# POOL's waits placed between shorter runs of the routing, and the second layer's bias products put into rounds of the expert loop

## The chip, the cores and the metric

The kernel runs on one core of one Trainium2 chip. The metric is the time of one execution in device microseconds; three runs are timed and the median counts. A profile is one execution recorded by the hardware profiler, with its own time. Engines are named as in the profile: PE (TensorE, matrix products), PEld (its weight loads), DVE (VectorE), ACT (ScalarE), POOL (GpSimd) and SP (SyncE, here only transfers and waits). All are programmed one by one and wait for each other through semaphores, counters that one engine raises and another waits on.

## What is computed

The input x is 128 x 125 x 64 (f32). Three stages follow one another; every number is f32 in the reference. Cut to what matters:

```python
h = tok(x)                        # depthwise conv, 5 taps, stride 2: 128 x 63 x 64; norm; leaky relu
h = h + attn(layernorm(h))        # selective scan, 16 states, along 63 positions
# third stage: 64 experts, 2 of them per token (8064 tokens)
xf = layernorm(h).reshape(-1, 64)
logits = xf @ Wr + br
topk_logits, topk_idx = top_k(logits, 2)
gates = softmax(topk_logits, axis=1)
combine = zeros(T, 64); combine[token, topk_idx] += gates
for e in range(64):
    y = relu(xf @ W1[e] + b1[e]) @ W2[e] + b2[e]
    out = out + combine[:, e:e + 1] * y
h = h + out
```

Since every y carries b2[e], the bias part of the output is `combine @ b2`, an 8064 x 64 by 64 x 64 product.

## The kernel before, in words

The first two stages take some 390 us and are not touched. The third one works on 63 tiles of 128 tokens, one tile per position. A tile has 128 rows of 64 numbers, one token in each partition.

**Routing.** The tiles are cut into groups of 8 (group 0 to 7) and into three shares: groups 0 and 1, groups 2 to 4, groups 5 to 7. For each group ACT normalises, PE transposes and multiplies by Wr (L762, L767), ACT copies the logits (L1117), DVE takes the two best experts (`choose`, L1504 to L1511, which raises s_hot). PE then counts tokens per expert (L807, L811; ACT copies the counts, L1123) and ranks each token within its expert (L823, L825, L833). At a share's end DVE works out where each expert's rows begin (`offsets_of`, s_off), PE adds these (L841, s_rank), and DVE turns ranks into row numbers, the slots (L1533 to L1547, s_slot). POOL then scatters the rows: for each tile and each of its two choices one indirect transfer (`send`, L630) writes 128 rows of the tile to `sorted_rows`, 126 transfers in all. They are numbered d = 0 to 125; share 0 has d = 0 to 31, share 1 d = 32 to 79, share 2 d = 80 to 125.

**The expert loop.** The sorted rows are padded to 40 units of 4 pairs of 128-row tiles. A step takes 2 pairs; there are 80 steps (24, 28 and 28 in the shares). In round k PE computes the output products of step k - 4 (L906), the hidden products of step k - 2 (L897) and the transposes of the rows of step k (L887), and then raises s_pstep. ACT and DVE wait for that round: ACT copies the transposed rows (L1162) and applies relu to half of the hidden part (L1167), DVE to the other half (L1595) and copies the outputs (L1604); they raise s_astep and s_dstep. PE's round k waits for their round k - 2. ACT stores the outputs of a step to `expert_out` (L1176); SP loads the weights of the pairs ahead into 23 places.

**The gathers.** For each tile and choice POOL fetches the 128 results by an indirect gather (L651), 126 in all, numbered d = 126 to 251; a share's gathers wait for all its stores. The last share's 46 gathers lie behind the loop. DVE then multiplies by the gates and adds (L1645, L1647), and SP writes the output.

**The bias part.** Beside the loop DVE builds the combine matrix (L1612, L1622). Behind the loop, for each of 8 groups q, PE transposes four 128 x 128 blocks of it (L940), ACT copies them (L1213), PE multiplies them by b2 (L931) and DVE adds the result to h (L1653, raising s_cbc).

**POOL's waits.** `keep_pace(d)` is called ahead of every indirect transfer. Three tables say where POOL waits: `GROUP_AT` (for s_hot, the choices of a group), `STEP_AT` (for a step of the loop, at every second transfer from d = 62 on, spread so that 153 transfers go with 80 steps) and `BIAS_AT` (for s_cbc, at every third transfer from d = 212 on). They set how POOL's transfers lie beside the other engines' work, and are not needed for the data.

Of the kernel before, what the change touches and what calls it, by code (L numbers as in the profile page):

```python
# [15 lines left out]
P = 128  # L16
T_IN = 125
C = 64
# [47 lines left out]
LAG_H, LATE = 2, 4  # L66
STEPS = [-(-n // 2) for n in PAIRS]
# [50 lines left out]
def groups_of(h):  # L118
    a, z = SHARES[h]
    return range(a // QG, -(-z // QG))  # L120

# [21 lines left out]
def build(nc, x, w, b, gamma, beta, alpha, A_log, D_param, scale, W_dt, b_dt, W_B, b_B, W_C, b_C,  # L143
# [5 lines left out]
    with ExitStack() as ctx:  # L149
# [88 lines left out]
        xT_e = x_w1[:, o:o + 4 * P].rearrange("p (k q n) -> p k q n", k=2, n=P)  # L238
        o += 4 * P
# [102 lines left out]
        s_comb = sem("s_comb")  # L342
        s_cT = sem("s_cT")
        s_cTc = sem("s_cTc")
        s_cb = sem("s_cb")
        s_cbc = sem("s_cbc")
# [112 lines left out]
        def _(pool):  # L459
# [197 lines left out]
        def _(pe):  # L657
# [223 lines left out]
            def rows_T(i):  # L881

                for j, n in enumerate(pairs_of(i)):
                    u = unit_of(n)
                    if in_share(n) % UNIT == 0:
                        pe.wait_ge(s_rows[u % RING], 16 * (u // RING + 1))
                    last = pe.transpose(ps[:, i % 2, j * P:(j + 1) * P], rows_in[:, u % RING, in_share(n) % UNIT, :],  # L887
                                        ident[:, :])
                return last

            def hidden(i):
# [3 lines left out]
                for j, n in enumerate(pairs_of(i)):  # L895
                    for t in range(2):
                        last = pe.matmul(ps[:, 2 + 2 * (i % 2) + t, j * P:(j + 1) * P],  # L897
                                         w_of(n)[t * C:(t + 1) * C, t, 0:HID],
                                         xT_e[t * C:(t + 1) * C, i % 2, j, :], start=True, stop=True)
# [10 lines left out]
            for k in range(STEP0[-1] + LATE):  # L910
                if k >= LAG_H:
                    pe.wait_ge(s_astep, k - LAG_H + 1)
# [3 lines left out]
                if LAG_H <= k < STEP0[-1] + LAG_H:  # L916
# [5 lines left out]
            pe.wait_ge(s_b2, 32)  # L922
            pe.wait_ge(s_dstep, dve_rounds(STEP0[-1]))

            def bias_of(q):

                pe.wait_ge(s_cTc, q + 1)
                if q >= 2:
                    pe.wait_ge(s_cbc, q - 1)
                for j in range(4):  # L930
                    last = pe.matmul(ps[:, 4 + q % 2, j * P:(j + 1) * P], cT[:, q % 2, j * P:(j + 1) * P], b2w[:, :],  # L931
                                     start=True, stop=True)
                last.then_inc(s_cb, 1)

            for q in range(CQ):
                pe.wait_ge(s_comb, q + 1)
                if q >= 2:
                    pe.wait_ge(s_cTc, q - 1)
                for j in range(4):
                    last = pe.transpose(ps[:, q % 2, j * P:(j + 1) * P],  # L940
                                        comb[0][:, 8 * q + 2 * j:8 * q + 2 * j + 2, :].rearrange("p l e -> p (l e)"), ident[:, :])
                last.then_inc(s_cT, 1)
                if q > 0:
                    bias_of(q - 1)
            bias_of(CQ - 1)

        @block.scalar
        def _(act):
# [210 lines left out]
            def xT_copy(i):  # L1159

                m = len(pairs_of(i))
                return act.activation(xT_e[:, i % 2, 0:m, :].rearrange("p q n -> p (q n)"), ps[:, i % 2, 0:m * P], ACT.Copy)  # L1162
# [23 lines left out]
            def next_rows(i):  # L1186

                d = i + 1
                u = d // (UNIT // 2) - 1 + RING
                if d % (UNIT // 2) == 0 and u < UNIT0[-1]:  # L1190
                    rows_of_unit(u)
# [3 lines left out]
            for k in range(STEP0[-1] + LAG_H):  # L1195
                act.wait_ge(s_pstep, k + 1)
                if k < STEP0[-1]:
                    last = xT_copy(k)
                if k >= LAG_H:
                    last = relu_A(k - LAG_H)  # L1200
                last.then_inc(s_astep, 1)
                if k < STEP0[-1]:
                    next_rows(k)
# [4 lines left out]

            for q in range(CQ):
                act.wait_ge(s_cT, q + 1)  # L1210
                if q >= 2:
                    act.wait_ge(s_cb, q - 1)
                act.activation(cT[:, q % 2, :], ps[:, q % 2, :], ACT.Copy).then_inc(s_cTc, 1)  # L1213

        @block.vector
        def _(dve):
# [401 lines left out]
            def both_gates(q):  # L1618
# [3 lines left out]
                dve.tensor_tensor(comb[0][:, span, :], comb[0][:, span, :], comb[1][:, span, :], ALU.add  # L1622
                                  ).then_inc(s_comb, 1)
# [59 lines left out]
```

## Time and profile before

| | us |
|---|---|
| median of 3 runs | 845.22 (843.47 to 846.76) |
| the profiled execution, its own time | 847.63 |
| its span | 845.7 |
| PE busy | 500.7 (59%) |
| DVE busy | 559.6 (66%) |
| ACT busy | 323.1 (38%) |
| POOL busy | 597.6 (71%) |

The mean granted TensorE clock was 0.778 of full speed. The span is the time from the first to the last instruction on the profiler's clock; the execution's own time is 1.9 us longer. In a row of the timeline the first number is the start in us from the span's start, the second how long it took; then come engine, line, operation, written tile, read tiles and shapes; x8 at the end means eight instructions in one row. In brackets stands how long the engine had been idle and what ended that. "remote" or "another core or an unknown queue" stands where no work was found that ended a wait; "issue" where no wait is seen. A PE product of f32 data shows as two passes, so 4 products show as x8; a transpose shows as one pass.

### The profile page before, as it was taken

How to read it: one execution, taken by the hardware profiler on the slowest of the kernel's cores; microseconds unless marked ns; L12 is line 12 of the kernel's file. 1: busy time of each engine (PE TensorE's matmuls, PEld its weight loads, DVE VectorE, ACT ScalarE, POOL GpSimd, SP SyncE). 2: the span in 40 equal slices, each digit the busy share in tenths (PEclk: the TensorE clock that was granted, in tenths of full speed). 3: DMA queues.
4: the chain of work that ended last, by engine and by line, in shares of the span. 5: the costliest groups of instructions: out<-in, count | busy, mean ns of one | idle time of the engine just before them, and what ended most of it. 6: DMA issues, size and time to landing. Idle time of an engine off the chain costs nothing.

```text
span 845.7 us, 8932 instructions
## 1 busy us (share of the span) xinstructions
PE 500.7 (59%) x2514; PEld 323.0 (38%) x2520; DVE 559.6 (66%) x1180; ACT 323.1 (38%) x622; POOL 597.6 (71%) x393
## 2 busy tenths in 40 slices
PE   4744245657558576556644675776886784777200
PEld 4733012222223122223423252665675673666100
DVE  1697899999999999997823564444544552333082
ACT  2159856555646655542310230222322331332000
POOL 5995779999999999992272357466666546654664
PEclk9968568798878879887756575799979895998555
DMA  7999970000000000000035102588888995852121
GB/s 251 382 183 121 77 3 0 1 0 0 0 0 0 0 0 0 0 0 0 8 91 141 30 19 89 148 230 248 234 254 234 250 289 133 232 148 58 23 84 51
DMA packets 106604, 84.95 MB, mean 100 GB/s; under 512 B 30464, under 2 KB 90240, under 8 KB 106560
## 3 DMA queue, kind: packets, MB, share of 16 engines
q1 hardware_dynamic: 79312, 54.76, 30.1%
q10 hardware_dynamic: 19184, 21.40, 8.6%
q0 software_dynamic: 8064, 8.27, 3.9%
q8 instruction: 19, 0.31, 0.2%
q14 instruction: 25, 0.20, 0.1%
HBM read 57.22 MB, written 33.49 MB: 107 GB/s over the span
## 4 chain that ended last, share of the span: by engine, by line
POOL 29%; PE 28%; issue 13%; DVE 11%; another core or an unknown queue 10%; ACT 6%; DMA 1%; ACTq 1%; POOLq 1%; DVEq 0%
POOL x_w L578 14%; POOL w_ring L571 10%; PE ps L906 10%; PE ps L897 6%; PE ps L887 5%; POOL xt L651 2%; PE ps L740 1%; PE ps L767 1%; PE ps L762 1%; DVE x_w L1595 1%; ACT xp L1102 1%; POOL hg L491 1%; POOL hh_ring L488 1%; DVE lstat L1290 1%
## 5 line engine op out<-in xcount | busy, mean ns | idle before, releaser
L740 PE MATMUL ps<-x_w,ident 128*128 128x512 f32 x252 | 154.9, 774 | 99.7 <-POOL x_w L578 99.7
L630 POOL DMA_INDIRECT sorted_rows<-xp,slot_i x126 | 122.4, 971 | 115.9 <-issue 34.7
L651 POOL DMA_INDIRECT xt<-expert_out,slot_i x126 | 121.9, 967 | 80.9 <-issue 31.7
L571 POOL TENSOR_TENSOR w_ring<-xt,bc 128x2016 f32<-128x2016 f32 x32 | 143.9, 4499 | 13.4 <-DVE hh_ring L1419 7.3
L1419 DVE TENSOR_TENSOR_SCAN hh_ring<-ps,w_ring 128x1024 f32<-128x1024 f32 x64 | 145.7, 2277 | 0.1
L578 POOL TENSOR_TENSOR x_w<-hh_ring,bc 128x2016 f32<-128x2016 f32 (+1 forms) x32 | 141.5, 4424 | 1.2 <-PE ps L740 1.2
L740 PEld LDWEIGHTS ps<-x_w,ident 128*128 128x128 f32 x252 | 60.5, 250 | 196.7 <-POOL x_w L578 122.6
L1162 ACT ACTIVATE x_w<-ps 128x256 f32<-128x256 f32 x80 | 30.8, 386 | 184.6 <-PE ps L887 129.1
L1072 ACT ACTIVATE ps<-dt_t,a_exp 128x1024 f32<-128x1024 f32 x64 | 71.5, 1117 | 64.3 <-DVE hh_ring L1419 64.3
L1066 ACT ACTIVATE ps<-dt_t,a_exp 128x1024 f32<-128x1024 f32 x64 | 71.5, 1118 | 51.2 <-DVE w_ring L1398 51.2
L1398 DVE TENSOR_TENSOR w_ring<-ps,w_ring 128x1008 f32<-128x1008 f32 x64 | 76.5, 1196 | 4.2 <-ACT ps L1066 4.2
L1413 DVE SCALAR_TENSOR_TENSOR w_ring<-ps,w_ring 128x1008 f32<-128x1008 f32 x64 | 75.5, 1179 | 0.0
L1595 DVE TENSOR_SCALAR x_w<-ps,x_w 128x128 f32<-128x128 f32 x56 | 17.3, 345 | 63.2 <-remote 31.6
L906 PE MATMUL ps<-dt_t,x_w 128*128 128x128 f32 x280 | 44.2, 305 | 25.0 <-DVE x_w L1604 14.1
L1595 DVE TENSOR_SCALAR x_w<-ps,dt_t 128x128 f32<-128x128 f32 x70 | 21.5, 345 | 53.7 <-PE ps L887 50.2
L906 PE MATMUL ps<-x_w 128*128 128x128 f32 x224 | 37.0, 315 | 32.7 <-DVE x_w L1604 12.4
L906 PEld LDWEIGHTS ps<-dt_t,x_w 128*128 128x128 f32 x280 | 39.1, 215 | 28.6 <-ACT x_w L1167 24.9
L906 PEld LDWEIGHTS ps<-x_w 128*128 128x128 f32 x224 | 33.3, 226 | 35.1 <-ACT x_w L1167 23.8
L887 PE MATMUL ps<-ident,x_w 128*128 128x128 f32 x160 | 38.1, 324 | 0.4 <-issue 0.4
L1604 DVE COPY x_w<-ps 128x256 f32<-128x256 f32 x80 | 33.2, 415 | 0.9 <-PE ps L906 0.8
L740 PE MATMUL ps<-hh_ring,ident 128*128 128x512 f32 x16 | 10.9, 822 | 33.5 <-ACT hh_ring L1055 26.0
L1595 DVE TENSOR_SCALAR x_w<-ps,bc 128x128 f32<-128x128 f32 x34 | 10.6, 345 | 25.3 <-PE ps L887 21.2
(209 smaller groups left out, 920.1 us busy)
## 6 DMA issues: line engine op xcount, KB each, us to landing
dt_t<-packed SPq DMA_DIRECT2D x140, 96.5 KB
x_w<-packed SPq DMA_DIRECT2D x112, 96.5 KB
x_w<-sorted_rows ACTq DMA_DIRECT2D x40, 256.0 KB
expert_out<-x_w ACTq DMA_DIRECT2D x80, 128.0 KB
sorted_rows<-pad_rows SPq DMA_DIRECT2D x2, 3584.0 KB, 24.1
bc<-packed SPq DMA_DIRECT2D x68, 96.5 KB
packed<-in_L_ffn_W SPq DMA_DIRECT2D x3, 2048.0 KB, 42.0
x_w<-in_x SPq DMA_DIRECT2D x7, 448.0 KB, 8.6
```

The costliest lines, as they stand in the source:

```text
L571: pool.tensor_tensor(w_buf(k, 2), up3[:, bass.ds(c * DC, DC), 1:S].unsqueeze(1).broadcast_to([P, 2, DC, L]), vec_of(k, 2), ALU.mult).then_ ...
L578: pool.tensor_tensor(hc_buf(k, n), h_buf(k, n), vec_of(N + k, n), ALU.mult).then_inc(s_hcp, n)
L630: pool.indirect_dma_start(out=sorted_rows[h], out_offset=bass.IndirectOffsetOnAxis(ap=slot_i[:, c, l:l + 1], axis=0), in_=xn[:, l, :], in_ ...
L651: pool.indirect_dma_start(out=y[:, l, :], out_offset=None, in_=expert_out[h], in_offset=bass.IndirectOffsetOnAxis(ap=slot_i[:, c, l:l + 1] ...
L740: ins = pe.matmul(ps[:, i, :], ident[:, :], src[:, i * BANK:(i + 1) * BANK], start=(k < 0), stop=(k == (N - 2 if last else N - 1)), skip_g ...
L887: last = pe.transpose(ps[:, i % 2, j * P:(j + 1) * P], rows_in[:, u % RING, in_share(n) % UNIT, :], ident[:, :])
L906: last = pe.matmul(ps[:, 6 + i % 2, (2 * j + t) * OUT:(2 * j + t + 1) * OUT], hT_e[:, i % 2, t, j, :], w_of(n)[:, t, HID + C - OUT:HID + C ...
L1066: act.activation(banks(6, 2), d, ACT.Tanh, scale=a_exp[:, 2, k:k + 1]).then_inc(s_th, 1)
L1072: act.activation(banks(2 + 2 * (k % 2), 2), d, ACT.Exp, scale=a_exp[:, 1, k:k + 1]).then_inc(s_dA, 1)
L1398: dve.tensor_tensor(wv, body(banks(6, 2)), wv, ALU.mult).then_inc(s_g, 1)
L1413: dve.scalar_tensor_tensor(out=wv, in0=body(dA), scalar=1.0, in1=wv, op0=ALU.add, op1=ALU.mult).then_inc(s_b, 1)
L1419: dve.tensor_tensor_scan(hh_ring[:, k % 4, :], dA, w_ring[:, k % 4, :], 0.0, ALU.mult, ALU.add).then_inc(s_h, 1)
```

## The change

Two things change.

*POOL's waits in the routing.* `GROUP_AT` has new places: the waits for groups 2, 3 and 4 (s_hot 3, 4, 5) stand at d = 6, 12 and 20 instead of 18, 21 and 25, those for groups 5, 6 and 7 at d = 40, 44 and 48 instead of 38, 41 and 44. A new table, `OFFSETS_AT`, makes POOL wait for the offsets of share 1 at d = 26 and of share 2 at d = 52.

*The bias part moves into the loop.* The rows of a whole unit (4 pairs) are now transposed at once in every even round, into one bank of PSUM, and copied by ACT in one instruction of twice the size. So the second bank comes free, and odd rounds have no row transposes. In round 13 + 8q PE transposes four blocks of the combine matrix into that bank (`gates_T`) and ACT copies them; in round 15 + 8q PE multiplies them by b2 into the same bank (`bias_of`) and DVE adds them to h (`add_bias`). The code behind the loop that did this, its five semaphores and `BIAS_AT` are gone. The first two rounds, which only had row transposes, become the transposes of unit 0 ahead of the loop.

```diff
+TURNED, ADDED = 13, 15
-GROUP_AT = {18: 3, 21: 4, 25: 5, 38: 6, 41: 7, 44: 8}
+GROUP_AT = {6: 3, 12: 4, 20: 5, 40: 6, 44: 7, 48: 8}
+OFFSETS_AT = {26: 2, 52: 3}
-BIAS_AT = {212 + 3 * q: q + 1 for q in range(CQ)}
+def group_at(k, first):
+    return (k - first) // 8 if k >= first and (k - first) % 8 == 0 and (k - first) // 8 < CQ else None
...
                 if d in GROUP_AT:
                     pool.wait_ge(s_hot, GROUP_AT[d])
+                if d in OFFSETS_AT:
+                    pool.wait_ge(s_off, OFFSETS_AT[d])
                 if d in STEP_AT:
                     pool.wait_ge(s_pstep, STEP_AT[d] + LATE)
-                if d in BIAS_AT:
-                    pool.wait_ge(s_cbc, BIAS_AT[d])
...
-            def rows_T(i):
+            def rows_T(u):
-                for j, n in enumerate(pairs_of(i)):
-                    u = unit_of(n)
-                    if in_share(n) % UNIT == 0:
-                        pe.wait_ge(s_rows[u % RING], 16 * (u // RING + 1))
-                    last = pe.transpose(ps[:, i % 2, j * P:(j + 1) * P], rows_in[:, u % RING, in_share(n) % UNIT, :],
-                                        ident[:, :])
+                pe.wait_ge(s_rows[u % RING], 16 * (u // RING + 1))
+                for q in range(UNIT):
+                    last = pe.transpose(ps[:, 0, q * P:(q + 1) * P], rows_in[:, u % RING, q, :], ident[:, :])
                 return last
...
+            def gates_T(q):
+                for j in range(4):
+                    last = pe.transpose(ps[:, 1, j * P:(j + 1) * P],
+                                        comb[0][:, 8 * q + 2 * j:8 * q + 2 * j + 2, :].rearrange("p l e -> p (l e)"), ident[:, :])
+                return last
+            def bias_of(q):
+                for j in range(4):
+                    last = pe.matmul(ps[:, 1, j * P:(j + 1) * P], cT[:, q % 2, j * P:(j + 1) * P], b2w[:, :],
+                                     start=True, stop=True)
+                return last
-            for k in range(STEP0[-1] + LATE):
-                if k >= LAG_H:
-                    pe.wait_ge(s_astep, k - LAG_H + 1)
+            pe.wait_ge(s_b2, 32)
+            rows_T(0).then_inc(s_pstep, 2)
+            for k in range(2, STEP0[-1] + LATE):
+                pe.wait_ge(s_astep, k - LAG_H + 1)
...
-                if k < STEP0[-1]:
-                    last = rows_T(k)
+                if k % 2 == 0 and k < STEP0[-1]:
+                    last = rows_T(k // 2)
+                if group_at(k, TURNED) is not None:
+                    last = gates_T(group_at(k, TURNED))
+                if group_at(k, ADDED) is not None:
+                    last = bias_of(group_at(k, ADDED))
                 last.then_inc(s_pstep, 1)
...
-            for k in range(STEP0[-1] + LAG_H):
+            act.wait_ge(s_pstep, 2)
+            xT_copy(0).then_inc(s_astep, 2)
+            next_rows(0)
+            for k in range(2, STEP0[-1] + LAG_H):
                 act.wait_ge(s_pstep, k + 1)
-                if k < STEP0[-1]:
-                    last = xT_copy(k)
-                if k >= LAG_H:
-                    last = relu_A(k - LAG_H)
-                last.then_inc(s_astep, 1)
+                if k % 2 == 0 and k < STEP0[-1]:
+                    xT_copy(k // 2)
+                if group_at(k, TURNED) is not None:
+                    cT_copy(group_at(k, TURNED))
+                relu_A(k - LAG_H).then_inc(s_astep, 1)
...
+            def add_bias(q):
+                n = min(8, L - 8 * q)
+                h = hg[:, 8 * q:8 * q + n, :]
+                return dve.tensor_tensor(h, ps[:, 1, 0:n * C].rearrange("p (l d) -> p l d", d=C), h, ALU.add)
...
                 if k >= LATE:
                     last = y_copy(k - LATE)
+                if group_at(k, ADDED) is not None:
+                    last = add_bias(group_at(k, ADDED))
                 last.then_inc(s_dstep, 1)
```

On POOL, in the routing of share 0, from the fourth row of its scatters on (the rows are the indirect scatters with the semaphore that the first of them waits for; `-` is before, `+` is now, rows without a sign stand in both; before, the first 17 scatters and the wait for group 1's slots stand ahead of these rows):

```order
-L630 DMA sorted_rows<-xp,slot_i 12288x64
+L630 DMA sorted_rows<-xp,slot_i 12288x64 x5
 L630 DMA sorted_rows<-xp,slot_i 12288x64 [waits s_hot]
-L630 DMA sorted_rows<-xp,slot_i 12288x64 x2
+L630 DMA sorted_rows<-xp,slot_i 12288x64 x5
 L630 DMA sorted_rows<-xp,slot_i 12288x64 [waits s_hot]
 L630 DMA sorted_rows<-xp,slot_i 12288x64 x3
+L630 DMA sorted_rows<-xp,slot_i 12288x64 [waits s_slot]
+L630 DMA sorted_rows<-xp,slot_i 12288x64 x3
 L630 DMA sorted_rows<-xp,slot_i 12288x64 [waits s_hot]
-L630 DMA sorted_rows<-xp,slot_i 12288x64 x6
+L630 DMA sorted_rows<-xp,slot_i 12288x64 x5
+L630 DMA sorted_rows<-xp,slot_i 12288x64 [waits s_off]
+L630 DMA sorted_rows<-xp,slot_i 12288x64 x5
```

The waits for choices come after 6 and 12 transfers instead of 18 and 21, and one for the offsets stands six transfers behind the third.

On PE, in rounds 37 to 39 of the expert loop, first before (L906 outputs, L897 hidden, L887 row transposes):

```order
L906 MATMUL ps<-bc,x_w 128x128 x4
L897 MATMUL ps<-x_w 128x128 x4
L887 MATMUL ps<-ident,x_w 128x128 x2
L906 MATMUL ps<-bc,x_w 128x128 x2
L906 MATMUL ps<-x_w 128x128 x2
L897 MATMUL ps<-x_w 128x128 x4
L887 MATMUL ps<-ident,x_w 128x128 x2
L906 MATMUL ps<-x_w 128x128 x4
L897 MATMUL ps<-x_w 128x128 x4
L887 MATMUL ps<-ident,x_w 128x128 x2
```

and now (L903 outputs, L894 hidden, L885 row transposes, L910 the transposes of the combine matrix, L917 the bias products):

```order
L903 MATMUL ps<-bc,x_w 128x128 x4
L894 MATMUL ps<-x_w 128x128 x4
L910 MATMUL ps<-ident,us_lg 128x128 x4
L903 MATMUL ps<-bc,x_w 128x128 x2
L903 MATMUL ps<-x_w 128x128 x2
L894 MATMUL ps<-x_w 128x128 x4
L885 MATMUL ps<-ident,x_w 128x128 x4
L903 MATMUL ps<-x_w 128x128 x4
L894 MATMUL ps<-x_w 128x128 x4
L917 MATMUL ps<-b2w,w_ring 128x128 x4
```

Rounds 37 and 39 have lost their two row transposes and have four transposes or four products in their place; round 38 has four row transposes instead of two.

On POOL, the first gathers behind the last share's stores, before:

```order
L651 DMA xt<-expert_out,slot_i 128x64
L651 DMA xt<-expert_out,slot_i 128x64 [waits s_cbc,s_pstep]
L651 DMA xt<-expert_out,slot_i 128x64 x2
L651 DMA xt<-expert_out,slot_i 128x64 [waits s_cbc]
L651 DMA xt<-expert_out,slot_i 128x64 x2
L651 DMA xt<-expert_out,slot_i 128x64 [waits s_cbc]
```

and now:

```order
L651 DMA xt<-expert_out,slot_i 128x64
L651 DMA xt<-expert_out,slot_i 128x64 [waits s_pstep]
L651 DMA xt<-expert_out,slot_i 128x64 x39
```

The waits for the bias groups are gone, and 39 gathers stand in one row behind the last wait for a step.

## Rows read from the trace of the kernel before

**Rows 1.** Page, chain that ended last: shares of the span by engine.

```profile
POOL 29%; PE 28%; issue 13%; DVE 11%; another core or an unknown queue 10%; ACT 6%; DMA 1%; ACTq 1%; POOLq 1%; DVEq 0%
```

**Rows 2.** Chain of waits in order of time: start us, us, what.

```profile
431.65 20.68 another core or an unknown queue
```

**Rows 3.** Timeline, POOL, routing: start us, us, operation, idle before.

```profile
416.81 1.17 POOL L630 DMA_INDIRECT sorted_rows<-xp,slot_i  x1 [21.45 <-DVE slot_i L1547]
...
445.96 0.97 POOL L630 DMA_INDIRECT sorted_rows<-xp,slot_i  x1 [2.50 <-issue]
...
449.78 0.97 POOL L630 DMA_INDIRECT sorted_rows<-xp,slot_i  x1 [0.30 <-issue]
...
483.98 0.97 POOL L630 DMA_INDIRECT sorted_rows<-xp,slot_i  x1 [12.00 <-DVE slot_i L1547]
...
498.72 0.97 POOL L630 DMA_INDIRECT sorted_rows<-xp,slot_i  x1 [3.57 <-DVE hh_ring L1511]
...
505.20 0.97 POOL L630 DMA_INDIRECT sorted_rows<-xp,slot_i  x1 [2.96 <-DVE hh_ring L1511]
...
526.87 0.97 POOL L630 DMA_INDIRECT sorted_rows<-xp,slot_i  x1 [0.30 <-issue]
```

**Rows 4.** Timeline of DVE, PE and ACT in the routing.

```profile
424.51 1.23 DVE L1511 TENSOR_TENSOR hh_ring<-ps,top 128x1024 bf16<-128x1024 f32 x1
...
429.01 0.63 PE L811 MATMUL ps<-hh_ring,squares 128*128 128x64 bf16 x8
...
452.36 0.28 ACT L1123 ACTIVATE counts<-ps 128x128 bf16<-128x128 f32 x1 [20.71 <-remote]
...
461.87 1.22 DVE L1511 TENSOR_TENSOR hh_ring<-ps,top 128x1024 bf16<-128x1024 f32 x1
...
523.50 0.69 PE L887 MATMUL ps<-ident,x_w 128*128 128x128 f32 x2
...
530.83 0.38 ACT L1162 ACTIVATE x_w<-ps 128x256 f32<-128x256 f32 x1 [9.88 <-remote]
```

**Rows 5.** DMA of 431.65 to 452.36: instruction packets, MB, share; loads issued.

```profile
q14 instruction: 1, 0.01, 0.2%
...
x_w<-packed SPq DMA_DIRECT2D x8, 96.5 KB
```

**Rows 6.** Timeline of the loop: ACT, POOL and PE.

```profile
724.25 0.38 ACT L1162 ACTIVATE x_w<-ps 128x256 f32<-128x256 f32 x1 [3.54 <-PE ps L887]
...
728.26 0.95 POOL L651 DMA_INDIRECT xt<-expert_out,slot_i  x1 [0.30 <-issue]
...
730.34 0.38 ACT L1162 ACTIVATE x_w<-ps 128x256 f32<-128x256 f32 x1 [4.32 <-PE ps L887]
...
730.50 0.44 PE L887 MATMUL ps<-ident,x_w 128*128 128x128 f32 x2
...
731.21 0.38 ACT L1162 ACTIVATE x_w<-ps 128x256 f32<-128x256 f32 x1
```

**Rows 7.** Windows: stretch, us, busy us (x) of PE, PEld, DVE, ACT, POOL.

```profile
684.00:692.00 8.00, 8.00 (x80) 6.93 (x78) 5.85 (x21) 3.60 (x12) 0.04 (x1) 1.00 1.06 323
```

**Rows 8.** Timeline behind the loop: bias products and POOL's gathers.

```profile
773.60 0.69 DVE L1653 TENSOR_TENSOR hg<-ps,hg 128x512 f32<-128x512 f32 x1 [0.64 <-PE ps L931]
...
774.03 0.60 ACT L1213 ACTIVATE w_ring<-ps 128x512 f32<-128x512 f32 x1 [0.73 <-PE ps L940]
...
774.73 0.60 PE L940 MATMUL ps<-ident,us_lg 128*128 128x128 f32 x4
...
775.16 1.06 PE L931 MATMUL ps<-b2w,w_ring 128*128 128x128 f32 x8
...
781.45 2.08 PE L931 MATMUL ps<-b2w,w_ring 128*128 128x128 f32 x8 [3.46 <-issue]
...
800.91 0.96 POOL L651 DMA_INDIRECT xt<-expert_out,slot_i  x1 [2.55 <-DVEq L1654]
...
807.33 0.95 POOL L651 DMA_INDIRECT xt<-expert_out,slot_i  x1 [2.94 <-DVEq L1654]
```

More of the change, by code:

```diff
@@ L898, in hidden @@
                                          w_of(n)[t * C:(t + 1) * C, t, 0:HID],
-                                         xT_e[t * C:(t + 1) * C, i % 2, j, :], start=True, stop=True)
+                                         xT_e[t * C:(t + 1) * C, i // 2 % 2, 2 * (i % 2) + j, :], start=True, stop=True)
                 return last
@@ L915, in _ @@
                     last = outputs(k - LATE)
-                if LAG_H <= k < STEP0[-1] + LAG_H:
+                if k < STEP0[-1] + LAG_H:
                     last = hidden(k - LAG_H)
-                if k < STEP0[-1]:
-                    last = rows_T(k)
-                last.then_inc(s_pstep, 1)
[L922 to L945, printed above, removed]
+                if k % 2 == 0 and k < STEP0[-1]:
[4 more added lines that the diff above has]
+                    last = bias_of(group_at(k, ADDED))
+                last.then_inc(s_pstep, 1)
         @block.scalar
@@ L1156, in _, with xT_copy, cT_copy @@
             act.activation(top[:, 1, :], top[:, 0, :], ACT.Exp).then_inc(s_eexp, 1)
-            def xT_copy(i):
-                m = len(pairs_of(i))
-                return act.activation(xT_e[:, i % 2, 0:m, :].rearrange("p q n -> p (q n)"), ps[:, i % 2, 0:m * P], ACT.Copy)
+            def xT_copy(u):
+                return act.activation(xT_e[:, u % 2, :, :].rearrange("p q n -> p (q n)"), ps[:, 0, :], ACT.Copy)
+            def cT_copy(q):
+                return act.activation(cT[:, q % 2, :], ps[:, 1, :], ACT.Copy)
             def relu_A(i):
@@ L1184, in rows_of_unit, with next_rows @@
                 load_rows(act, u)
[L1186 to L1191, printed above, removed]
+            def next_rows(u):
+                if u + RING < UNIT0[-1]:
+                    rows_of_unit(u + RING)
             for v in range(RING):
                 rows_of_unit(v)
-            for k in range(STEP0[-1] + LAG_H):
+            act.wait_ge(s_pstep, 2)
+            xT_copy(0).then_inc(s_astep, 2)
+            next_rows(0)
+            for k in range(2, STEP0[-1] + LAG_H):
                 act.wait_ge(s_pstep, k + 1)
-                if k < STEP0[-1]:
-                    last = xT_copy(k)
-                if k >= LAG_H:
-                    last = relu_A(k - LAG_H)
-                last.then_inc(s_astep, 1)
-                if k < STEP0[-1]:
-                    next_rows(k)
+                if k % 2 == 0 and k < STEP0[-1]:
[3 more added lines that the diff above has]
+                relu_A(k - LAG_H).then_inc(s_astep, 1)
+                if k % 2 == 0 and k < STEP0[-1]:
+                    next_rows(k // 2)
                 if k > LATE:
@@ L1207, in _ @@
                 store(i)
[L1209 to L1213, printed above, removed]
         @block.vector
@@ L1621, in both_gates @@
                 dve.wait_ge(s_dve, ch.at)
-                dve.tensor_tensor(comb[0][:, span, :], comb[0][:, span, :], comb[1][:, span, :], ALU.add
-                                  ).then_inc(s_comb, 1)
+                dve.tensor_tensor(comb[0][:, span, :], comb[0][:, span, :], comb[1][:, span, :], ALU.add)
             for k in range(2):
                 ch.link(dve.memset(comb[k][:, L, :], 0.0))
+            def add_bias(q):
+                n = min(8, L - 8 * q)
+                h = hg[:, 8 * q:8 * q + n, :]
+                return dve.tensor_tensor(h, ps[:, 1, 0:n * C].rearrange("p (l d) -> p l d", d=C), h, ALU.add)
             for k in range(LAG_H, STEP0[-1] + LATE):
@@ L1647, in gate_rows @@
                 return dve.tensor_tensor(hg[:, span, :], hg[:, span, :], y[:, span, :], ALU.add)
-            for q in range(CQ):
-                n = min(8, L - 8 * q)
-                h = hg[:, 8 * q:8 * q + n, :]
-                dve.wait_ge(s_cb, q + 1)
-                ch.link(dve.tensor_tensor(h, ps[:, 4 + q % 2, 0:n * C].rearrange("p (l d) -> p l d", d=C), h, ALU.add))
-                dve.sem_inc(s_cbc, 1)
             for g in range(len(OUTS)):
```

9 lines of the change are left out of this document (2 added, 7 removed).

## The prediction

> **What bounds the kernel now.** I read the page first, then the chain of waits in order of time, then the timeline of each engine around its longest pieces, last the expert loop step by step. The chain gives 10% of the span to "another core or an unknown queue" and 13% to "issue" [rows 1]. There is one core, so the first name only means that no work was found that ended those waits. Its longest piece is 20.68 us from 431.65 [rows 2].
>
> Look at what goes on beside it. PE ends the count products of group 2 at 429.01 + 0.63 = 429.64; ACT, whose next instruction waits for that count alone, starts it at 452.36, after 20.71 us of idling [rows 4]. POOL issues row transfers all the while: 21 in one run from 416.81 to 443.46, then from 445.96 to 449.78 + 0.97 = 450.75, and then it stops [rows 3]. ACT moves 1.6 us after that stop. The same before the loop: PE ends the transposes of a step at 523.50 + 0.69 = 524.19, ACT gets them at 530.83 [rows 4], and POOL's run has ended at 526.87 + 0.97 = 527.84 [rows 3]. So: **while POOL sends its indirect transfers one behind the other, PE's signals can be held, and they come through when POOL pauses**. That is read from times, not from a record of the signals.
>
> The expert loop obeys the same rule. ACT takes two steps at 724.25 and the next two at 730.34, 6.09 us later; POOL's fourth transfer between them ends at 728.26 + 0.95 = 729.21, 1.1 us before [rows 6]. While POOL stands still (684 to 692) PE runs 80 passes in 8.0 us [rows 7]; a step is 18 of them (8 outputs, 8 hidden, 2 transposes), so it takes 1.8 us there against 3.05 in the pairs. In most of the loop POOL sets the pace: two transfers to about one step, by the step waits in keep_pace.
>
> Behind the loop POOL gathers the last 46 tiles, and only the last sums and the output follow. What stops POOL there is on the path.
>
> **Part 1, POOL's waits in the routing.** Nothing is computed anew; the places of the pauses move, and two waits for offsets are added. POOL's transfers follow at 1.275 us ((526.87 - 505.20) / 17) [rows 3]. Queued behind each new wait are only further row transfers; who waits for them is the loop's loads of rows, much later.
>
> *Share 1's first groups.* Now POOL stops after 6 transfers, at about 424.4, until group 2's choice ends at 424.51 + 1.23 = 425.74 [rows 4]; a second stop comes after 12, at 426.0 + 5 x 1.275 + 0.97 = 433.3, for group 3's choice. If signals are held by then, this stop frees them as the one at 450.75 did: ACT copies the counts at 433.3 + 1.5 = 434.8 instead of 452.36, 17.5 us sooner. But the work from there to group 4's choice took 461.87 + 1.22 - 452.36 = 10.7 us with POOL standing, and now 8 transfers (10.2 us) lie over it. If none of its signals is held, all 17.5 us stay. If they are held to that run's end (about 446.7, so 448.2), with some 9 us of the 10.7 still to do, 6 us stay. I take **-10**, nearer the second end, since the weight loads that ran beside the 20 us stall [rows 5] run there too.
>
> *Between group 4's choice and share 1's slots.* Before, 7 transfers stood here, now 6, a wait for the offsets, and 6: 12 x 1.275 = 15.3 against 8.9 us. If a rank signal is held to the end of that run it comes 6.4 us later; if the middle wait pauses POOL, the run before it is one transfer shorter than the 7, and a hold ends 1.3 us sooner. I take **0**, nearer the second end, since the first needs the middle wait to be met while a signal is held, and keep both.
>
> *Share 2 and the loop's start.* From the slots at 483.98, POOL paused 3.57 and 2.96 us at its 42nd and 45th transfer [rows 3]. The waits now stand at the 45th and 49th: POOL comes to the 45th at 483.98 + 12 x 1.275 = 499.3, after that choice is done (498.72), and to the 49th at 504.4, when 0.8 us are missing (505.20). So transfer 62 starts at 483.98 + 29 x 1.275 + 0.8 = 521.8, not at 526.87, and the next thing is a step wait that the held step must pass. The hold ends with POOL's run: **-5.1**, up to -6.6 if the signal then goes through at once (530.83 - 524.19), and 0 if the longer run holds a signal of share 2's ranks.
>
> **Part 2, the bias products.** Out of the end go 8 groups of 4 transposes, a copy, 4 products and an addition, with the waits that POOL had on them. POOL lost 2.55 - 0.30 and 2.94 - 0.30 us on these [rows 8], together **-4.9**. The rest of that work hid behind gathers. Late next is POOL alone, 46 gathers in a row: the ends are -4.9 and, if VectorE's sums were held until the gathers end, a few groups of sums late: four instructions of about 0.69 us [rows 8] for each of two or three groups, +7. I take -4.9: before, VectorE did its sums beside 22 unbroken gathers from 807.33 on.
>
> Into the loop go, in each of 8 pairs of rounds, PE 0.60 + 1.06, ACT 0.60, VectorE 0.69 us [rows 8]. Row transposes go four to an even round instead of two to each, and ScalarE's copies likewise: no more work, and the odd rounds, lighter by two transposes, take the new products. What hides them is POOL: at 730.34 the first of two steps came through, while PE finished the second only at 730.50 + 0.44 = 730.94 [rows 6], and the pair was no longer than the others. ACT started the second at 731.21, 0.87 us after the first [rows 6], so PE may end about 0.9 us behind POOL's release for nothing; at full clock it ends earlier still. Only steps that run while POOL stands, and an addition in the first step of a pair, pay. Below: 0 (the coarser copies could even save a few tenths per pair, but POOL's pace takes them). Above: all in line, 8 x 2.95 = +23.6. I take **+2**, one group in the stretch without POOL (1.7) and little else.
>
> **Sum**: -10 + 0 - 5.1 - 4.9 + 2 = -18.0. The profiled execution took 847.6 us, so 829.6; the median of the runs shown is 2.4 below it: **827 us**.
>
> **Rivals.** (B) *The holds move with the runs.* Part 1 wins its lower end and share 1's ranks are held longer: -6 + 6.4 - 5.1 - 4.9 + 2 = -7.6, about 838. For it: in the loop runs of four transfers, 5 us, are enough to hold. Against: the run from 505.20 had gone on for 19 us when the loop's signal of 524.19 was held, and had let the ranks of share 2 through. (C) *Nothing is held any more* in the routing: -17.5 - 1.3 - 6.6 - 4.9 + 0 = -30.3, 815. Against it speak the loop's pairs, where runs of four already hold. (D) *The loop pays for the bias work*, slower. If the extra rounds fall out of step with POOL and PE falls to its lower clock, the products cost 2.08 us [rows 8] and the transposes likewise twice 0.60, so a group is 2.1 + 1.2 + 0.6 + 0.7 = 4.6 and eight are 36.8: -20.0 + 36.8 = +16.8, 862. It decides from (20.0 + 4.2) / 8 = 3.0 us per group. For it: PE is the longest of the engines in a step. Against: the pair at 724 had slack with PE slow. (E) *The stalls are fetches of instructions, not held signals*, so that moving POOL's waits does nothing: then only the end and the loop change, -4.9 + 2 = -2.9, about 842. For it: in the 20 us stall there is one packet on the queue named "instruction" [rows 5]. Against: one packet can't fill 20 us, and ACT moves when POOL stops [rows 3, 4]. [...]
>
> **How the numbers follow.** The forecast (A) has 0.58, B 0.17, C 0.08, D 0.10, E 0.07. What this measurement can tell from no change is 0.5%, 4.2 us, so 841 to 849.5 counts as the same. Faster: A, C and most of B, 0.80. Same: E and a rest of B, 0.10. Slower: D, 0.10. A's own range, with its bounds, is 820 to 835. For 8 in 10 the range takes in B, C and E and leaves out D and the outer ends of the others: 813 to 843.
>
> **What would show it.** In the new trace ACT's copy of group 2's counts starts near 435, not 452; the wait from 520 lasts under 5 us; POOL's last 46 gathers have no pause; the pairs of steps in the loop are still 6.1 us apart, those with bias work too, and the loop ends about 13 us sooner. I am wrong if the copy is still held over 10 us, if pairs with bias work stretch by a microsecond or more, or if VectorE's sums stand still under the last gathers and finish late.

## The result and the profile after

The changed kernel takes 836.87 us, median of 5 runs (835.33 to 838.26), against 845.22 (843.47 to 846.76): ratio 0.990, 95% interval 0.9871 to 0.9929. That is 8.35 us less, where 18.2 were forecast, and inside the range. The profiled execution took 836.15 us (before 847.63), its span is 834.3 us (before 845.7).

On the page the chain has changed owners against [rows 1]: the wait with no releaser fell from 10% to 5% of the span, "issue" grew from 13% to 16%.

```profile
PE 27%; DVE 20%; POOL 19%; issue 16%; ACT 8%; another core or an unknown queue 5%; SPq 1%; ACTq 1%; DMA 0%; POOLq 0%; DVEq 0%
```

In the timeline of POOL after (answers to [rows 3]) the first share's run is cut by pauses, share 1's slots come at 470.33 instead of 483.98, and the first pause behind them comes only after 12 transfers, before 486.36:

```profile
426.43 0.97 POOL L630 DMA_INDIRECT sorted_rows<-xp,slot_i  x1 [1.67 <-DVE hh_ring L1500]
...
436.75 0.97 POOL L630 DMA_INDIRECT sorted_rows<-xp,slot_i  x1 [3.00 <-DVE hh_ring L1500]
...
458.84 0.97 POOL L630 DMA_INDIRECT sorted_rows<-xp,slot_i  x1 [3.21 <-DVE first_tile L1511]
...
470.33 0.97 POOL L630 DMA_INDIRECT sorted_rows<-xp,slot_i  x1 [4.17 <-DVE slot_i L1536]
...
486.36 0.97 POOL L630 DMA_INDIRECT sorted_rows<-xp,slot_i  x1 [1.08 <-DVE hh_ring L1500]
...
490.17 0.97 POOL L630 DMA_INDIRECT sorted_rows<-xp,slot_i  x1 [0.30 <-issue]
...
500.69 0.96 POOL L630 DMA_INDIRECT sorted_rows<-xp,slot_i  x1 [9.55 <-DVE hh_ring L1500]
...
526.52 0.96 POOL L630 DMA_INDIRECT sorted_rows<-xp,slot_i  x1 [8.35 <-PE ps L885]
```

The timeline of ACT, DVE and PE after (answers to [rows 4]; ACT's L1114 is the old L1123):

```profile
435.06 0.28 ACT L1114 ACTIVATE counts<-ps 128x128 bf16<-128x128 f32 x1 [3.01 <-remote]
...
449.80 0.28 ACT L1114 ACTIVATE counts<-ps 128x128 bf16<-128x128 f32 x1 [8.30 <-remote]
...
478.14 0.63 PE L811 MATMUL ps<-hh_ring,squares 128*128 128x64 bf16 x8
...
484.65 0.18 DVE L1498 CAST top<-mi 128x16 f32<-128x16 uint32 x1 [3.69 <-remote]
...
489.67 0.28 ACT L1114 ACTIVATE counts<-ps 128x128 bf16<-128x128 f32 x1 [9.22 <-issue]
```

Group 2's counts are copied at 435.06 instead of 452.36. But in share 2 a stall stands that before did not have: PE ends group 5's counts at 478.77, and ACT, idle since 480.45, starts their copy at 489.67. In the kernel before, ACT was idle for only 0.52 us ahead of the same copy:

```profile
496.97 0.28 ACT L1123 ACTIVATE counts<-ps 128x128 bf16<-128x128 f32 x1 [0.52 <-remote]
```

Below, a signal is called held when the engine that waits for it starts long after the work that raises it has ended.

Four transfers of POOL cut the time into stretches that can be compared in every run: number 32 (first with share 1's slots), 62 (first under the loop's step waits), 206 (first gather behind the loop) and 251 (the last; the span ends 10.2 us later in each). The stretches are in us, from one profiled execution of each kernel. "Before there" is the median of the kernel before, run beside that kernel; the ratio is that of the two kernels' times. The rows below the first two are the experiments of the next section; they also explain what is meant by a chip with or without holds.

| kernel | 32 starts at | 32 to 62 | 62 to 206 | 206 to 251 | before there | ratio (95%) |
|---|---|---|---|---|---|---|
| before | 483.98 | 51.93 | 236.33 | 63.20 | | |
| after | 470.33 | 56.19 | 238.45 | 59.08 | 845.2 | 0.990 (0.987-0.993) |
| after, again, on a chip with holds | 469.69 | 55.71 | 235.50 | 59.51 | 841.5 | 0.988 (0.983-0.992) |
| share 2's old waits | 469.65 | 50.89 | 234.05 | 58.92 | 841.3 | 0.987 (0.983-0.992) |
| waits only | 472.86 | 54.94 | 237.32 | 59.84 | 841.3 | 0.991 (0.988-0.994) |
| bias part only | 482.59 | 51.54 | 235.05 | 58.62 | 841.3 | 0.999 (0.996-1.003) |
| POOL silent in share 2 | 489.78 | 42.57 | 235.66 | 58.68 | 841.3 | 1.001 (0.997-1.005) |
| no bias waits | 479.16 | 49.99 | 237.77 | 58.43 | 841.5 | 0.998 (0.994-1.002) |
| shorter runs in share 2 | 473.88 | 50.88 | 233.34 | 59.19 | 841.5 | 0.984 (0.980-0.988) |
| old waits, and one at 57 | 473.71 | 46.58 | 236.96 | 58.57 | 841.5 | 0.980 (0.976-0.984) |
| no bias work in the loop | 469.59 | 52.84 | 235.15 | 58.82 | 840.6 | 0.990 (0.986-0.994) |
| shorter runs, and one at 57 | 472.37 | 45.74 | 237.57 | 58.20 | 840.6 | 0.982 (0.978-0.985) |
| after, on a chip without holds | 460.12 | 38.15 | 183.97 | 57.71 | 752.9 | 1.000 (0.998-1.003) |

Ratios leave out slow executions, among them three of 12 without bias waits (855.62 to 857.51 us) and one of 12 with the bias part only (2270.98 us).

Between the two profiled executions the terms are -13.65, +4.26, +2.12 and -4.12, together -11.4, the difference of the spans. The medians differ by less since the profiled execution of before was 2.4 us above its median and that of after 0.7 below. Single profiles of kernels that do the same thing in a stretch differ by 3 us there (62 to 206 in the two runs of after), so smaller differences of one stretch are not read as effects.

### The profile page after: what moved, and what is told of

Read it like the earlier page. It is cut to its first block, busy times and chain, and to the rows that moved or that the text cites. A ratio compares the mean times of both kernels' runs of the same rounds, so it can differ in the third digit from the quotient of the medians.

```text
span 834.3 us, 8865 instructions
## 1 busy us (share of the span) xinstructions
PE 485.4 (58%) x2514; PEld 314.4 (38%) x2520; DVE 559.4 (67%) x1180; ACT 318.9 (38%) x582; POOL 597.6 (72%) x393
## 4 chain that ended last, share of the span: by engine, by line
PE 27%; DVE 20%; POOL 19%; issue 16%; ACT 8%; another core or an unknown queue 5%; SPq 1%; ACTq 1%; DMA 0%; POOLq 0%; DVEq 0%
PE ps L903 8%; POOL x_w L578 7%; POOL w_ring L571 6%; PE ps L894 6%; POOL xt L651 5%; DVE hh_ring L1408 4%; PE ps L885 3%; PE ps L676 2%; ACT ps L1057 2%; DVE w_ring L1402 2%; ACT ps L1063 2%; PE ps L740 2%; DVE w_ring L1387 2%; DVE x_w L1584 1%
## 5 line engine op out<-in xcount | busy, mean ns | idle before, releaser
L740 PE MATMUL ps<-x_w,ident 128*128 128x512 f32 x252 | 151.8, 760 | 102.4 <-POOL x_w L578 102.4
L1152 ACT ACTIVATE x_w<-ps 128x512 f32<-128x512 f32 x40 | 23.9, 597 | 145.0 <-remote 50.3
L903 PE MATMUL ps<-dt_t,x_w 128*128 128x128 f32 x280 | 43.7, 302 | 22.0 <-DVE x_w L1593 10.8
L903 PEld LDWEIGHTS ps<-dt_t,x_w 128*128 128x128 f32 x280 | 38.2, 210 | 26.3 <-issue 23.2
L903 PE MATMUL ps<-x_w 128*128 128x128 f32 x224 | 34.0, 296 | 20.8 <-issue 16.1
L903 PEld LDWEIGHTS ps<-x_w 128*128 128x128 f32 x224 | 29.6, 205 | 23.7 <-issue 19.7
L740 PE MATMUL ps<-hh_ring,ident 128*128 128x512 f32 x16 | 11.4, 852 | 33.3 <-ACT hh_ring L1046 26.1
L885 PE MATMUL ps<-ident,x_w 128*128 128x128 f32 x160 | 29.0, 307 | 1.9 <-issue 1.5
L894 PE MATMUL ps<-x_w,dt_t 64*128 64x128 f32 x280 | 28.0, 316 | 0.2 <-issue 0.2
```

Source lines behind the costliest of these rows:

```text
L740: ins = pe.matmul(ps[:, i, :], ident[:, :], src[:, i * BANK:(i + 1) * BANK], start=(k < 0), stop=(k == (N - 2 if last else N - 1)), skip_g ...
L903: last = pe.matmul(ps[:, 6 + i % 2, (2 * j + t) * OUT:(2 * j + t + 1) * OUT], hT_e[:, i % 2, t, j, :], w_of(n)[:, t, HID + C - OUT:HID + C ...
```

## The experiments

The expectations count groups by the value POOL waits for (3 to 8): their "group 6" is group 5 of the text above.

**Share 2's old waits** in the changed kernel:

```diff
-GROUP_AT = {6: 3, 12: 4, 20: 5, 40: 6, 44: 7, 48: 8}
-OFFSETS_AT = {26: 2, 52: 3}
+GROUP_AT = {6: 3, 12: 4, 20: 5, 38: 6, 41: 7, 44: 8}
+OFFSETS_AT = {26: 2}
```

> The changed kernel with the waits of share 2 put back where the kernel before has them: GpSimd waits for group 6 at transfer 38, group 7 at 41, group 8 at 44, and has no wait for share 2's slots at 52. Share 1's new waits and the bias rounds stay. Theory (GpSimd's run of 12 transfers, from 470.33 to 485.28 us in the profile after, has no pause in it, holds the counts of group 6 for 9.22 us, and the routing of share 2 ends later by it): the stretch from share 1's slots to the loop's second pair, 55.95 us after and 46.85 before, comes back to 45 to 48; the time is 9 to 11 us under that after, about 827 (ratio to before 0.976 to 0.981). Rival 1 (the stretch grew because of the new order of the loop's first rounds, not of the waits): it stays near 56 and the time stays at 837. Rival 2 (the 9 us go wherever share 1's earlier slots leave the transfers, a limit of the weight loads or of the stores): the stretch stays at 52 or more, 834 or more.

Timeline of this kernel, PE, ACT and POOL after share 1's slots:

```profile
477.50 0.63 PE L811 MATMUL ps<-hh_ring,squares 128*128 128x64 bf16 x8
...
482.46 0.28 ACT L1114 ACTIVATE counts<-ps 128x128 bf16<-128x128 f32 x1 [2.66 <-remote]
...
483.90 0.97 POOL L630 DMA_INDIRECT sorted_rows<-xp,slot_i  x1 [3.10 <-DVE hh_ring L1500]
```

POOL stops after 9 transfers, at 480.80, and the copy begins at 482.46, not 489.67. Stretch 32 to 62 falls from 56.19 and 55.71 to 50.89. Over all traces from chips with holds that keep share 2's old waits, and have no other wait added there, it is 49.99 to 51.93 us; with the new ones it is 52.84 to 56.19. ACT's idle time ahead of that copy is 0.41 to 2.66 us in the former and 4.51 to 9.22 in the latter. So the new waits of share 2 cost some 4 to 5 us of stretch, not the order of the loop's first rounds. In the times it shows less: the ratio is 0.987 where I expected 0.976 to 0.981, and its interval overlaps that of the changed kernel. I had sized the step by ACT's second pair (46.85 against 55.95 us); transfer 62, which the loop's pace hangs on, had moved by half of that.

**Each part alone.** The kernel before with the new tables of waits (and nothing else), and the changed kernel with the old tables:

```diff
+GROUP_AT = {6: 3, 12: 4, 20: 5, 40: 6, 44: 7, 48: 8}      # waits only: on the kernel before
+OFFSETS_AT = {26: 2, 52: 3}
```

> The kernel before with the new table of waits alone; the bias work stays behind the loop, and GpSimd waits for it there. Theory (each part acts by itself: share 1 gives 13.65 us, share 2 costs 9.1, the loop and the tail as before): 845.2 - 4.5 = 840.7 (838 to 843), ratio 0.995. Rival 1 (share 2's loss comes from the new order of the loop's first rounds): without it the waits alone give 13.65 + 5.1 us, 826. Rival 2 (what is gained ahead of the loop is lost in it): 845.

```diff
+GROUP_AT = {18: 3, 21: 4, 25: 5, 38: 6, 41: 7, 44: 8}     # bias part only: on the changed kernel
+OFFSETS_AT = {}
```

> The changed kernel with the old table of waits: only the bias work is in the loop, and the loop's rounds are in their new order. Theory: the loop gives 2.7 us (as between the two traces) and the tail 4.1, so 845.2 - 6.8 = 838.4 (836 to 841), ratio 0.992. Rival 1 (the new order costs at the loop's start): the stretch from share 1's slots to the loop's second pair grows from 46.85 to about 56, and the time is near 848. Rival 2 (the loop's 2.7 us came from its earlier or later start): 841.

The waits give 0.991, -7.6 us of 841.3, and the bias part 0.9993, -0.6 (-3.4 to +2.3). I had expected 0.995 and 0.992. They add up to the change's 0.990. The long stretch 32 to 62, 54.94 us, is there without the new order of the loop.

These kernels and the one with share 2's old waits ran on one chip, so their medians can be compared. New waits in both shares: 833.72 us. Share 2's old waits: 828.37. The old waits in both: 840.57. So share 1's new waits won 12.2 us (840.57 - 828.37). Share 2's new waits lost 5.4 (833.72 - 828.37), or 4.7 if the bias part, the other difference of those two kernels, is taken at its own 0.7 (841.27 - 840.57). The single runs of the two kernels overlap (828.80 to 837.20 and 825.61 to 833.90), so the second number is a rough one.

**POOL silent in share 2**: the same instructions, but POOL waits for all of share 2's slots ahead of transfer 32.

```diff
+GROUP_AT = {6: 3, 12: 4, 20: 5}
+OFFSETS_AT = {26: 2, 32: 3}
```

> The changed kernel, with GpSimd waiting for all of share 2's slots ahead of transfer 32, so that it issues nothing while share 2 is routed; what any engine executes, and in which order, is the same. It isn't meant to be fast: 30 transfers of 1.25 us start only then, about 850 us (842 to 865). Theory (what waits is a signal held behind GpSimd's transfers): ScalarE's copy of group 6's counts begins within 1 us of its release and of ScalarE being free, where it began 9.22 us late after; share 2's routing, from group 5's choice to its slots, runs without a wait over 3 us. Rival (that stall is an instruction fetch of ScalarE or TensorE at that place in the code): it stays, 5 us or more at the same line, since the code is the same.

Timeline of this kernel: PE's counts of group 5, ACT's copy, and POOL's first transfer after the silence.

```profile
476.62 0.64 PE L811 MATMUL ps<-hh_ring,squares 128*128 128x64 bf16 x8
...
478.83 0.27 ACT L1114 ACTIVATE counts<-ps 128x128 bf16<-128x128 f32 x1
...
489.78 0.97 POOL L630 DMA_INDIRECT sorted_rows<-xp,slot_i  x1 [25.07 <-DVE first_tile L1511]
```

The copy has no idle time before it. The same code at the same place stalls 9.22 us with POOL sending and not at all with POOL silent. That alone leaves one rival, a fetch of code that POOL's transfers slow down. The DMA view of the kernel after, over ACT's idle time (480.46 to 489.67), answers it. It lists one queue, that of POOL's own transfers, and no packet of the instruction queues:

```profile
q0 software_dynamic: 224, 0.23, 6.9%
```

It cost less than expected, 840.83 us (ratio 1.001) instead of 842 to 865: transfer 32 came 19.45 us later than in the kernel after (489.78 against 470.33), but 32 to 62 took only 42.57 us.

**On another chip.** The next four kernels, the changed one among them, ran on a chip where the kernel before takes 752.9 us.

> The changed kernel once more, beside the experiments. If the parts add up as they were measured alone (waits alone 0.991, bias alone 0.9993), its ratio to before is 0.990 again (0.987 to 0.993).

It took 752.37 us, ratio 1.0004 (0.9977 to 1.0031). Its timeline, PE and ACT in share 2, and POOL:

```profile
434.67 0.97 POOL L630 DMA_INDIRECT sorted_rows<-xp,slot_i  x1 [0.34 <-DVE hh_ring L1500]
...
464.50 0.45 PE L811 MATMUL ps<-hh_ring,squares 128*128 128x64 bf16 x8
...
466.70 0.26 ACT L1114 ACTIVATE counts<-ps 128x128 bf16<-128x128 f32 x1
...
516.06 0.97 POOL L630 DMA_INDIRECT sorted_rows<-xp,slot_i  x1 [0.30 <-PE ps L885]
```

From 434.67 to 516.06 POOL sends 65 transfers with no pause over 0.35 us, three times the run of 21 that held a signal for 20 us, and nothing is held: ACT copies the same counts with no idle time. The loop's stretch takes 183.97 us, 144 transfers at 1.278: POOL pauses only once there, for 0.75 us, and it is some 52 us shorter than on the other chips. So back-to-back transfers alone don't hold signals; the chip must be one on which they do. Seen over all runs: on three chips the kernel before took 840.6 to 841.5 us (845.2 in the first pair), on two 752.7 to 752.9, and the transfers themselves are as long on both (0.97 us). On those two the no-bias-waits kernel gave 1.0004, shorter runs 1.0019, the wait at 57 1.0013, no bias work 1.0015, and 1 lies in the interval of each; shorter runs with the wait at 57 gave 1.0043 (1.0019 to 1.0067), a small loss, as pauses that free nothing would give. The runs below are from chips with holds.

> The changed kernel once more, with the three runs that follow. The last four ran where the kernel before took 752.88 us and no version differed from it. If the kernel before takes some 840 us here: TensorE's signals are held as in the first traces, ScalarE's copy of group 6's counts comes 5 us or more late, and the ratio is 0.990 (0.987 to 0.993). If it takes some 753 us: no stall, ratio 1.000.

0.9876: the first result again. ACT's copy of group 5's counts is at 487.38 here, 7.54 us idle before it, while POOL's run goes on to 489.78:

```profile
487.38 0.28 ACT L1114 ACTIVATE counts<-ps 128x128 bf16<-128x128 f32 x1 [7.54 <-remote]
...
488.81 0.97 POOL L630 DMA_INDIRECT sorted_rows<-xp,slot_i  x1 [0.30 <-issue]
...
499.76 0.96 POOL L630 DMA_INDIRECT sorted_rows<-xp,slot_i  x1 [9.98 <-DVE hh_ring L1500]
```

So a held signal can also come through inside a run. The first trace had shown it too: there ACT's copy starts at 489.67 in a run of four transfers (486.36 to 491.14), 4.4 us after POOL's stop at 485.28, and DVE's CAST, held 3.69 us, starts at 484.65 before that stop. "When POOL pauses" is too simple.

This trace shows something more, which "held signals" does not describe. Group 4's choice ends at 442.50. The first row is that choice; then come products of PE (L807, the counts of group 4), with nothing to wait for from one to the next:

```profile
441.27 1.23 DVE L1500 TENSOR_TENSOR hh_ring<-ps,top 128x1024 bf16<-128x1024 f32 x1
...
450.49 0.27 PE L807 MATMUL ps<-hh_ring,squares 128*128 128x128 bf16 x1 [1.83 <-issue]
...
456.78 0.27 PE L807 MATMUL ps<-hh_ring,squares 128*128 128x128 bf16 x1 [1.11 <-issue]
```

The eight products take 10.13 us here, from 446.92 to 457.05, and 3.49 in the first trace of this kernel. In the kernel before, and on the chip without holds, they take 0.61:

```profile
441.49 0.61 PE L807 MATMUL ps<-hh_ring,squares 128*128 128x128 bf16 x8
```

In the other traces with share 1's new waits on chips with holds they take 4.89 to 9.44 us. So on these chips single instructions come late as well, although they wait for no semaphore, and even for 2 us after POOL's stop at 454.51. Why is open. No experiment here was made for it.

**No bias waits** in the kernel before:

```diff
-BIAS_AT = {212 + 3 * q: q + 1 for q in range(CQ)}
+BIAS_AT = {}
```

> The kernel before without GpSimd's waits for the bias work behind the loop. Where the kernel before takes some 840 us: as predicted (the waits cost their pauses) 4.9 us faster, ratio 0.994; what the run with the waits alone points to (0.8 us of pauses instead of 4.9 in the same place), 0.998 to 1.000; rival (VectorE's additions are held behind the unbroken gathers) 1.003 or more. Where it takes some 753 us: 1.000.

0.9981 (0.9944 to 1.0017), and POOL has no pause in the gathers behind the loop. The rival of late sums is out, and my -4.9 (0.994) lies just below the interval. With the bias waits still in (waits only), POOL's longest pause there is this one:

```profile
799.88 1.34 POOL L654 DMA_INDIRECT xt<-expert_out,slot_i  x1 [1.14 <-issue]
```

against 2.55 and 2.94 in [rows 8]. One execution had shown me pauses that another does not have.

**Shorter runs in share 2:**

```diff
+GROUP_AT = {6: 3, 12: 4, 20: 5, 35: 6, 39: 7, 45: 8}
+OFFSETS_AT = {26: 2, 48: 3}
```

> Share 2's waits at 35, 39, 45 and 48. Where the kernel before takes some 840 us: theory (runs of at most 6 transfers let TensorE's signals through) the stretch from transfer 32 to 62 is 47 to 50 us, where it was 56.19 after and 50.89 with the old waits, ratio 0.983 to 0.987; rival (each pause costs what it lets through) 52 us or more, 0.989 or more. Where it takes some 753 us: 1.000 to 1.002, as before.

828.70 us against 831.52 of the changed kernel on the same chip, ratio 0.984, as expected; the stretch, 50.88, is a little above the 47 to 50 expected. Group 5's counts and group 6's are no longer held. Group 7's are: its choice was done when POOL came to 45, so that wait gave no pause, and a run of 9 (486.30 to 497.43) went over the signal. PE, ACT and POOL in its timeline:

```profile
492.04 0.55 PE L807 MATMUL ps<-hh_ring,squares 128*128 128x128 bf16 x7
...
499.23 0.22 ACT L1114 ACTIVATE counts<-ps 128x64 bf16<-128x64 f32 x1 [10.63 <-remote]
...
500.68 0.96 POOL L630 DMA_INDIRECT sorted_rows<-xp,slot_i  x1 [3.25 <-DVE first_tile L1511]
```

**One wait at the loop's start.** In the kernel with share 2's old waits PE ended the row transposes of the second unit at 507.89. ACT, which copies them, started at 514.82, after POOL's run had ended at 513.45. (The 509 us of the expectation is the end of PE's next products, which this copy does not wait for.)

```profile
506.77 1.12 PE L885 MATMUL ps<-ident,x_w 128*128 128x128 f32 x4
...
512.48 0.97 POOL L630 DMA_INDIRECT sorted_rows<-xp,slot_i  x1 [0.30 <-issue]
...
514.82 0.60 ACT L1152 ACTIVATE x_w<-ps 128x512 f32<-128x512 f32 x1 [9.27 <-remote]
```

```diff
+                if d == 57:
+                    pool.wait_ge(s_pstep, 3)
```

> Share 2's old waits and a wait at transfer 57 for TensorE's step 3 of the loop. Where the kernel before takes some 840 us: theory (ScalarE and VectorE began 9.27 and 9.87 us late behind 18 unbroken transfers, and now begin within 1 us of TensorE's end) transfer 62 comes 45 to 47 us after transfer 32 instead of 50.89, ratio 0.980 to 0.983; rival (the earlier start is given back in the loop) 0.987 as without the wait. Where it takes some 753 us: 1.000.

With the wait (its lines stand two lower), PE, ACT and POOL:

```profile
511.67 1.11 PE L887 MATMUL ps<-ident,x_w 128*128 128x128 f32 x4
...
513.67 0.60 ACT L1154 ACTIVATE x_w<-ps 128x512 f32<-128x512 f32 x1 [3.21 <-PE ps L887]
...
513.91 0.97 POOL L632 DMA_INDIRECT sorted_rows<-xp,slot_i  x1 [2.48 <-PE ps L887]
```

PE ends the transposes at 512.78, within POOL's pause of 2.48 us, and the copy starts 0.89 us later instead of 6.93. 32 to 62 takes 46.58 us, and the time is 825.35 us (821.05 to 828.57), ratio 0.980: 6.2 us under the changed kernel on the same chip (827.75 to 834.89). Both lie in what was expected, and it beats the kernel before and the changed one.

**No bias work in the loop**: `gates_T`, `cT_copy`, `bias_of` and `add_bias` are not called (the second layer's bias is missing from the output); the rounds keep their new order.

> The changed kernel without the bias rounds' work (the output lacks the second layer's bias). Where the kernel before takes some 840 us: predicted cost of 2 us, ratio 0.986 to 0.988; no cost, as the traces point to, 0.988 to 0.990 (the changed kernel's own two ratios are 0.990 and 0.9876, so a cost under 3 us can't be told from none); a cost of 8 us or more, 0.980 or less.

0.9901 (0.9862 to 0.9939), where the changed kernel has 0.990 and 0.988: the bias rounds cost nothing that can be measured. A cost of 2 us, as forecast, would not stand out.

**Shorter runs and the wait at 57**, the latter as above:

```diff
+GROUP_AT = {6: 3, 12: 4, 20: 5, 35: 6, 39: 7, 42: 8}
+OFFSETS_AT = {26: 2, 45: 3}
```

> Share 2's waits at 35, 39, 42 and 45 and the wait at 57. Where the kernel before takes some 840 us: they add up, transfer 62 comes 44 to 47 us after transfer 32, ratio 0.976 to 0.981; they give the same microseconds twice, 47 to 49 us, 0.981 to 0.984. Where it takes some 753 us: 1.002 to 1.007, as the last run had it (1.0043).

The wait at 42 does let group 7's counts through (copy at 491.60), and 32 to 62 is 45.74 us. But the ratio is 0.982 (0.978 to 0.985), no better than with the wait at 57 alone. The stretch is what adding up would give and the ratio lies between the two expectations, so these runs don't decide between them.

## Why the prediction was wrong

The sign and the range held, and so did the mechanism in share 1's first groups; the size was off by more than half.

- *Share 1's first groups*, -10. The copy came at 435.06, 434.8 forecast. Group 4's choice ended at 448.03 instead of 463.09, 15.1 us sooner, and in the second trace at 442.50, 20.6 sooner: nearer the -17.5 end, and past it. The next signals were held as allowed for, 8.30 us of idling before group 3's copy (449.80), but not each for a whole run.
- *Between group 4's choice and share 1's slots*, 0. It took 20.89 us before and 22.30 after, so 1.4 were lost, and share 1's slots came 13.65 us sooner in all. In the second trace it took 27.2, and 25.56 to 27.23 in six others with the same waits (19.87 and 19.89 in two with the old ones). That is the size of the +6.4 that the working named and left out of its sum, but not the way it named: PE's products of group 4 came late one by one, and it was not a rank signal.
- **Share 2 and the loop's start, -5.1: the step that failed.** It counted when POOL would get to its waits, and took every other engine's times of share 2 as fixed. In the kernel before, the wait for group 6's choice at transfer 41 made POOL pause after 9 transfers (3.57 us before 498.72, [rows 3]), just as group 5's counts were ready. It now stands at 44, and the wait at 40 was met when POOL came (0.30 us of idling ahead of that transfer), so the run grew to 12 transfers and the pause that had let group 5's counts through was gone. Measured +4.26 in the stretch, 9.4 us from the forecast; the old waits gave back 5 there, and 5.4 in the medians on one chip. The working did name such a hold, and priced it at 0 as its upper end. It should have been the length of the run, as I had done for share 1 (+6.4). Corrected by this alone, -18.0 becomes -8.6. That this is so near the measured 8.35 is luck in part: share 1 gave 3.65 us more than forecast, the end some 3 to 4 less.
- *The end*, -4.9. Traces: -4.12 between the two; times: -0.6 for the whole bias part and -1.6 (-4.7 to +1.4) for the waits taken away alone. The step read two pauses of one execution as lasting; a second trace with these waits has one of 1.14 us. The -4.12 is mostly that one execution: 206 to 251 took 63.20 us in it, and 57.71 to 59.84 in all the others of the table.
- *Bias work in the loop*, +2: nothing measurable, though 2 us is within the intervals. The part has 0.9993, the kernel without the work 0.9901, and pairs of rounds that stay 6.10 us apart where the gates are turned (timeline of ACT after):

```profile
719.48 0.60 ACT L1152 ACTIVATE x_w<-ps 128x512 f32<-128x512 f32 x1 [4.45 <-PE ps L885]
...
725.58 0.60 ACT L1152 ACTIVATE x_w<-ps 128x512 f32<-128x512 f32 x1 [4.47 <-PE ps L910]
...
731.68 0.60 ACT L1152 ACTIVATE x_w<-ps 128x512 f32<-128x512 f32 x1 [3.99 <-remote]
```

- Of the rivals B, 838 us, came nearest in number and is half right: holds do move with the runs, and share 1's second half did lose. But share 1's first groups won more than B gave them, and the largest miss was in share 2, where B kept the same -5.1. C is out (ACT still waited 8.30 and 9.22 us). D is out too, since the bias work does not cost anything near 3 us per group. (The eight passes in 1.06 us of [rows 8] stood at a granted clock of 1.00, those in 2.08 us at 0.50.) E is out by the silent run, by the stall without a packet of instructions, and by the chips without holds, where the same code has no stall. The one packet of [rows 5] took 0.2% of the time of 16 engines over 20.7 us, which I put at 0.7 us of transfer (0.002 x 16 x 20.7).

## What to carry to other kernels

A wait that spaces out an engine's work helps only if it is not yet met when the engine comes to it: check each against the new times, look at what the old pauses had let through, and price the longest unbroken run that is left. Undo the change by parts on the same chip before believing a trace's stretch: one execution showed 5 us of pauses, and taking them out gained 1.6 (at most 4.7). And run a gain that rests on stalls without a releaser on more than one chip: here all of it, and the best version's 2% too, exist on some chips only.

## What was not expected of the hardware

- Whether signals are held depends on the chip: 753 against 841 us for the same kernel, with equal transfers of 0.97 us. On the slower chips the loop's 144 transfers take 233 to 238 us, on the faster 182.5 to 185.0. What differs in the chips was not found; no run here could show it.
- Nor is it settled what lets a signal through. In five traces POOL's pause began within 2.8 us of the end of group 5's count products, and ACT's copy began 1.6 to 1.8 us after POOL's stop (482.46 after 480.80 with share 2's old waits). But a pause of 2.50 us (to 445.96, [rows 3]), 13.8 us after the signal of 429.64, did not free it, and in several traces a signal came inside a run of transfers. What is shown is that with no transfers nothing was held in share 2, and that a pause of about 2.5 to 3.6 us set at a signal's rise let it through in these runs.
- On the chips with holds, instructions that wait for nothing can come late as well (PE's eight count products of group 4, 3.49 to 10.13 us instead of 0.61). So "held signals" names what was seen most, and not a cause.
